# Gate and up weights fetched piece by piece in the last mixer slot, block 1's token rows fetched with block 0's, and block 0's first slice placed behind the last scores

## The reference

```python
xn = layernorm(x)
q, k, v = silu(xn @ Wq.T), silu(xn @ Wk.T), silu(xn @ Wv.T)
f = log_sigmoid(xn @ Wf.T) / 8;  s = 1 - exp(f)
# pass 1: S = S * exp(f) + k s^T;  ok = q S;  qv = softmax(ok)
# pass 2: S = S * exp(f) + s v^T;  ov = qv S
o = silu(ov);  rms = o * rsqrt(mean(o * o) + 1e-5)
attn = (rms * g_w) @ Wo.T
# feed-forward: act_quant to 8 bits by the row's largest value, weight_quant to {-1, 0, 1} / scale
gate = silu(bitlinear(xn, w_gate));  up = bitlinear(xn, w_up)
ffn = bitlinear(gate * up, w_down)
out = x + attn + ffn
```

## Time and profile before

| | |
|---|---|
| median of 3 runs | 1513.44 us (1511.06 to 1515.44) |
| the profiled execution | 1519.48 us |
| its span on the slowest core (core 7) | 1517.9 us; the other cores 1485.6 to 1512.5 us |
| PE busy / weight loads / DVE / ACT / POOL | 89% / 46% / 57% / 43% / 13% |
| 16 DMA engines, the two larger queues | 48.2% (SP's) and 5.9% (POOL's) of the span |
| slot 14 on core 7 | 793.7 to 827.8 us |
| transition on core 7 | 827.8 to about 892.4 us, where `down(0)` begins |
| feed-forward blocks behind it | 892.4 to 1517.9 us |

### The profile page before, as it was taken

How to read it: one execution, slowest core, us unless ns; L and a number is a source line. 1 busy time by engine, 2 the same in 40 slices (tenths; PEclk the granted TensorE clock), 3 DMA queues, 4 the chain that set the end, 5 groups by cost and what they waited for, 6 DMA issues and landing times.

```text
span 1517.9 us, 24194 instructions; the slowest of 8 cores (1485.6 to 1517.9 us)
## 1 busy us (share of the span) xinstructions
PE 1358.4 (89%) x7996; PEld 701.5 (46%) x7996; DVE 867.5 (57%) x1475; ACT 651.4 (43%) x1082; POOL 195.8 (13%) x225
## 2 busy tenths in 40 slices
PE   2666899878889988888898899999999999999999
PEld 1223344345556555555555344444444444444444
DVE  2455556338776667777777355554455445555543
ACT  1555322457788887877775211111111111111120
POOL 1000000011221111211212011111111011001110
PEclk9899999989999999999999999999999999999999
DMA  9898999716676766676752932323322233332322
GB/s 152 203 213 183 226 251 277 209 33 192 196 225 231 200 177 198 193 215 204 230 175 71 352 97 57 77 63 77 76 56 64 70 77 77 77 72 61 77 49 56
DMA packets 193690, 219.69 MB, mean 145 GB/s; under 512 B 125856, under 2 KB 146336, under 8 KB 192416
## 3 DMA queue, kind: packets, MB, share of 16 engines
q1 hardware_dynamic: 187664, 197.18, 48.2%
q0 software_dynamic: 5904, 20.97, 5.9%
HBM read 167.78 MB, written 29.36 MB: 130 GB/s over the span
## 4 chain that ended last, share of the span: by engine, by line
PE 64%; DMA 13%; DVE 8%; ACT 7%; issue 6%; SPq 2%; POOL 1%; DVEq 0%; ACTq 0%; POOLq 0%
PE ps L265 62%; DMA stg<-wgT 4%; DMA stg<-wuT 3%; DMA xin<-xp 2%; DMA wf<-wfT 2%; ACT b_ok L282 1%; SPq L310 1%; PE ps L270 1%; DVE STf L299 1%; ACT stg L282 1%; DVE part L418 1%; DMA xin<-xr 1%; DVE b_ok L285 1%; DVE stB L461 1%; ACT b_wo L282 1%
## 5 line engine op out<-in xcount | busy, mean ns | idle before, releaser
L265 PE MATMUL ps<-wgu,xnTb 128*128 128x512 fp8e4 x2048 | 447.3, 380 | 6.8 <-DVE gu L285 6.8
L265 PEld LDWEIGHTS ps<-wgu,xnTb 128*128 128x128 bf16 x2048 | 200.4, 98 | 248.8 <-issue 9.2
L282 ACT ACTIVATE sg<-ps,ccol 128x512 f32<-128x512 f32 x128 | 86.0, 684 | 424.1 <-PE ps L265 423.0
L265 PE MATMUL ps<-wd,qT 128*128 128x512 fp8e4 x960 | 209.6, 379 | 0.0
L285 DVE TENSOR_TENSOR gu<-ps,sg 128x512 f32<-128x512 f32 x128 | 88.3, 690 | 187.9 <-PE ps L265 178.7
L265 PEld LDWEIGHTS ps<-wd,qT 128*128 128x128 bf16 x960 | 94.0, 98 | 113.2
L282 ACT ACTIVATE stg<-stg,wsc 128x1024 f32<-128x1024 f32 x96 | 109.7, 1145 | 38.8 <-DMA stg<-wuT 17.3
L461 DVE TENSOR_SCALAR stB<-stg 128x1024 fp8e4<-128x1024 f32 x96 | 69.1, 719 | 67.7 <-ACT stg L282 59.1
L418 DVE TENSOR_REDUCE part<-stg 128x1 f32<-128x1024 f32 x64 | 77.5, 1218 | 48.6 <-DMA stg<-wgT 28.4
L265 PE MATMUL ps<-wf,xnTa 128*128 128x512 bf16 x256 | 65.4, 415 | 39.4 <-DMA wf<-wfT 27.4
L303 POOL CAST b_s<-STf 128x512 bf16<-128x512 f32 x64 | 45.7, 716 | 421.7 <-DVE STf L299 419.8
(11 more groups left out here) (139 smaller groups left out, 1933.8 us busy)
## 6 DMA issues: line engine op xcount, KB each, us to landing
stg<-wgT SPq DMA_DIRECT2D x64, 512.0 KB, 6.8
stg<-wuT SPq DMA_DIRECT2D x64, 512.0 KB, 6.2
stg<-wdT SPq DMA_DIRECT2D x64, 512.0 KB, 5.1
xin<-xr SPq DMA_DIRECT2D x32, 512.0 KB, 4.6
xin<-xp SPq DMA_DIRECT2D x16, 512.0 KB, 5.8
gu_s<-stB SPq DMA_DIRECT2D x64, 128.0 KB, 5.7
at_s<-b_wo SPq DMA_DIRECT2D x32, 256.0 KB, 2.2
wgu<-gu_s POOLq DMA_DIRECT2D x8, 1024.0 KB, 17.4
```

Source lines behind the costliest of these rows:

```text
L265: return pe(lambda e: e.matmul(out=out, lhsT=lhsT, rhs=rhs, start=start, stop=stop, skip_group_check=True), *toks, mark=mark)
L282: return sc(lambda e: e.activation(out=out, in_=in_, func=func, **kw), *toks)
```

## The change

Four edits, all around slot 14 and the transition:

1. `wv` and `wq` change places in memory, so that the four weights lie in the order in which slot 14 last reads them: `wf`, `wk`, `wq`, `wv`.
2. The eight loads of `wgu` are issued in four pairs in slot 14, each behind the last reader of the weight that lies there: slices 0 and 1 after `F_(15, 1)`, 2 and 3 after `K_(15, 1)`, 4 and 5 after `Q_(15, 1)`, 6 and 7 after `V_(15, 1)`. `F_`, `K_` and `Q_` record their last matmul as `wdone` for this.
3. `load_x(1)` moves from the transition to slot 14, right behind `load_x(0)`.
4. `gu_pe(0, 0)` moves from behind `Wo_pe(14, 1)` to directly behind `AT_(15)`.

`prep_x(1)`, which reads the rows that `load_x(1)` fetches, stays where it was.

```diff
--- before.py
+++ after.py
@@ -188,8 +188,8 @@
 
         wf = at("wf", 8192, BF16, W0)
         wk = at("wk", 8192, BF16, W0 + 16384)
-        wv = at("wv", 8192, BF16, W0 + 32768)
-        wq = at("wq", 8192, BF16, W0 + 49152)
+        wq = at("wq", 8192, BF16, W0 + 32768)
+        wv = at("wv", 8192, BF16, W0 + 49152)
         wgu = at("wgu", 65536, FP8, W0)
         wo = at("wo", 8192, BF16, WO0)
 
@@ -742,7 +742,7 @@
         def F_(c, h):
             d = B[c]
             bk = RP.take()
-            p = proj(c, bk, wf, wf_t, h)
+            d["wdone"] = p = proj(c, bk, wf, wf_t, h)
             u = U.get(("e", h))
             t = act(b_e[h], bk.ap, AF.Exp, p, u, A2_done, scale=-1.0)
             bk.put(t)
@@ -813,6 +813,7 @@
                            wq[:, kc * 1024 + col:kc * 1024 + col + 128],
                            xT[:, kc * 128:(kc + 1) * 128], kc == 0, kc == 7,
                            X[("o", c)]["xnT"], wq_t, bk.freed, mark=(kc == 7 and j == 3))
+            d["wdone"] = p
             t = act(b_QT[:, hsl(h)], bk.ap, AF.Silu, p, U.get(("QT", h)))
             bk.put(t)
             d["Q%d" % h] = t
@@ -820,7 +821,7 @@
         def K_(c, h):
             d = B[c]
             bk = RP.take()
-            p = proj(c, bk, wk, wk_t, h)
+            d["wdone"] = p = proj(c, bk, wk, wk_t, h)
             t = act(heads(b_KV[:, h * 1024:(h + 1) * 1024], 2, 0), v3(bk.ap, 2), AF.Silu, p,
                     U.get(("U", h)))
             bk.put(t)
@@ -1083,6 +1084,13 @@
         V = {}
         wl_t = []
         wd_t = []
+
+        def load_gu(g, tok):
+
+            for sl in (2 * g, 2 * g + 1):
+                wl_t.append(dma("wl%d" % sl, gp, wgu[:, sl * 8192:(sl + 1) * 8192],
+                                d_gu[:, sl * 8192:(sl + 1) * 8192], tok,
+                                store_t[0], store_t[1]))
 
         def load_x(b):
             s = b % 2
@@ -1234,6 +1242,8 @@
             up(c, 0)
             ok_ex(c, 1)
             F_(f, 1)
+            if s == NO - 2:
+                load_gu(0, B[f]["wdone"])
             qt_dv(c, 0)
             if w is not None:
                 Wo_pe(w, 0)
@@ -1273,6 +1283,7 @@
             if s == NO - 2:
                 bg_end = [stg_tok, stB_tok]
                 load_x(0)
+                load_x(1)
                 prep_x(0)
             K_(f, 0)
             bg_a()
@@ -1287,6 +1298,8 @@
             s2_cast(2)
             s2_cast(3)
             K_(f, 1)
+            if s == NO - 2:
+                load_gu(1, B[f]["wdone"])
             bg_a()
             bg_b()
             Q_(f, 0)
@@ -1295,6 +1308,8 @@
             bg_b()
             s1_tr(1, RC)
             Q_(f, 1)
+            if s == NO - 2:
+                load_gu(2, B[f]["wdone"])
             bg_a()
             bg_b()
             KT_(f, 1)
@@ -1302,6 +1317,8 @@
             bg_a()
             bg_b()
             V_(f, 1)
+            if s == NO - 2:
+                load_gu(3, B[f]["proj"])
             bg_a()
             bg_b()
 
@@ -1309,11 +1326,8 @@
         c = NO - 1
         w = c - 1
         upd_end = [("pe", pe.n), ("dv", dv.n), ("sc", sc.n), ("gp", gp.n)]
-        for sl in range(8):
-            wl_t.append(dma("wl%d" % sl, gp, wgu[:, sl * 8192:(sl + 1) * 8192],
-                            d_gu[:, sl * 8192:(sl + 1) * 8192], B[c]["proj"],
-                            store_t[0], store_t[1]))
         AT_(c)
+        gu_pe(0, 0)
         gram(w)
         ok_pe(c, 0)
         ok_dv(c, 0)
@@ -1328,7 +1342,6 @@
         Wo_el(w, 1)
         qt_dv(c, 1)
         wd_t.append(dma("wd", gp, wd, d_wd, store_t[2], B[c]["qt1"], upd_end))
-        gu_pe(0, 0)
         qT_(c, 0)
         BT_(c, 0)
         qT_(c, 1)
@@ -1337,7 +1350,6 @@
         ov_pe(c, 0)
         BT_(c, 1)
         ov_el(c, 0)
-        load_x(1)
         prep_x(1)
         gu_pe(0, 2)
         gu_el(0, 1)
```

## The result

The changed kernel takes 1507.58 us (median of 6 runs) against 1515.88 us before (6 runs), at a ratio of 0.9934 with an interval of 0.9914 to 0.9955, which is 10 us of 1515.88. Measured again beside the last experiments, it is 0.9946 (0.9925 to 0.9967), 8 us. 1505.6 us had been forecast, in a range of 1502.5 to 1510.5.

What follows compares the result with a forecast made beforehand. PE, busy 621.8 of 625.5 us from down(0) on, was taken to bound the kernel, so down(0)'s start sets its end. 6.48 + 1.64 - 0.3 = 7.8 us off the median 1513.4 gave 1505.6 us, range 1502.5 to 1510.5.

Steps and rivals of the forecast that it cites:

- The stall of slice 3: Before slice 3's up half, PE's idle 6.85 us shrinks to 1.19 us; gain 6.48 us, with slice 0's 0.66 us in it.
- The clock: Slice 3's up half, eight matmuls, runs at full clock after the shorter stall: 1.64 us more, bounds 0 to 1.64.
- Rival B: At slice 3 the clock stays low and some wait stays: gain 6.2 or 4.5 us, 1508 us; chance 0.17.
- Slice 0 ahead of `gram`: Its sixteen matmuls, moved ahead of gram and pass 1, cover the wait for mask b_at: 0.66 us gained.
- All of this costs nothing: Slices and wd, fetched from slot 14 on, land before PE wants them and delay nothing on POOL: 0 us.
- the slip of 0.3 us: Block 0's rows in slot 14 land 0.3 us late, which DVE's queue hands on to PE.
- almost done: The first pair, 2.1 MB in 6.1 us from 799.7, has nearly landed when block 0's rows are issued.
- a bound of 2.1 us: With turns by packet, block 0's rows take at most about twice 3.5 us in slot 14 and slip 2.1 us.
- rival C: No change: block 0's rows in slot 14 land 9.4 us late instead; 1514.7 us, chance 0.15.
- The reason given for the late rows: Block 1's rows took 14.28 us because their load shares the DMA engines with 12 MB of wgu and wd.
- even shares: Queues taking equal turns by packet; doubted because block 1's rows were a tenth of what moved in 14.28 us.
- D: Slower: slice 0, heading PE's queue, waits for block 0's transpose, 1 us per us beyond 828.25; 1518 us, chance 0.05.

Runs made afterwards that it cites:

- e1_rows_early: The kernel before with only load_x(1) moved, directly behind load_x(0) in slot 14; ratio 0.9975 to before.
- e4_slice0_back: The changed kernel with gu_pe(0, 0) put back behind Wo_pe(14, 1); 1511.88 us in one run.
- the six kernels: Those that fetch the first pair of slices early and leave prep_x(0) in its place; slot 14 takes 35.68 us on their mean.
- e6_pair0_later: The changed kernel with the first pair of slices issued together with the second, behind K_(15, 1); 1505.58 us in one run.
- e2_weights_early: The changed kernel with load_x(1) back in the transition and gu_pe(0, 0) back behind Wo_pe(14, 1); ratio 1.0034 to before.
- e8_wd_pieces: e2_weights_early with wd fetched as 8 loads with rows of 4 KB instead of one with rows of 32 KB; 1513.24 us in one run.
- e9_preps_later: The changed kernel with prep_x(0) moved to ahead of Q_(15, 0) and prep_x(1) to behind gu_el(0, 1); ratio 0.9988 to before.
- e10_slices_behind_transpose: e9_preps_later with slices 2 to 7 also waiting for block 0's transpose to land; ratio 0.9887 to before, 1498.20 us.

## Why the prediction was right, and where it was not

**The stall of slice 3: right.** On core 7, on which the sum was made, the transition went from 64.65 to 56.44 us, 8.2 us; 6.48 + 1.64 = 8.12 had been summed. The up half was due at 843.12 + 1.73 = 844.85 and began at 845.95, so 1.10 us stayed, where 1.19 had been worked out. `e1_rows_early` shows that the early rows alone remove the stall.

**The clock: right.** 0.94 us of idle time left eight matmuls at 1.89 us and the window at 1.00. Other runs show that it was not a near thing: 1.94 us cost nothing either, while 2.73 us cost most of the price (3.02 us), 4.42 us nearly all of it (3.38 us) and 14.14 us no more (3.27 us). Rival B did not come about.

**Slice 0 ahead of `gram`: right**, 0.66 us, shown by `e4_slice0_back`.

**"All of this costs nothing", and the slip of 0.3 us: the mechanism was right, the term of the sum was too small.** On five cores `prep_x(0)` started later than its queue let it, which the prediction had named as a sign of being wrong. Block 0's rows were late by 0.72 us on the mean (0 to 1.59; up to 2.62 on one core of the repetition), and slot 14 grew by 0.65 us, by 0.9 on the mean of the six kernels. The first pair of slices did it, shown by `e6_pair0_later`; it was not "almost done" as 6.1 us of bytes had it. The two loads took a median of 7.9 us from their issue, and the issue itself came about 0.8 us behind the last matmul of `F_(15, 1)`. The prediction had worked out a bound of 2.1 us from turns by packet and set it aside; the largest slip in the change's own profile was 1.59 us. With means over all cores the sum is 7.48 - 0.65 = 6.8 us, on the last core of before 8.2 less its slip. (In rival C a load of 8 us comes 3.1 us late, not 3.3.)

**The reason given for the late rows was wrong in kind.** The prediction laid it on 12 MB in flight, and held against even shares that the rows were a tenth of what was moved. The shares are even, but by packets: 132 to 162 while the bytes stood 7 to 1 (`e2_weights_early`), 197 to 197 in the kernel before, and the same bytes in shorter rows let the load through in about half the time (`e8_wd_pieces`). The rows were a tenth of what was moved because the stores ahead of them in SP's queue were another tenth, and the neighbour's packets were longer. The Trainium skill's rule on Arbitration ("DMA: Bandwidth & Descriptors") says just this, that a DMA engine goes round its queues packet by packet, and these runs agree with it. That the forecast stood all the same is in part luck: nothing in the reason given said what the rows would meet in slot 14, and they met only the tail of the first pair, with rows of 8 KB. It follows from turns by packet that the early weights don't relieve the rows' load: without `load_x(1)` beside them they make it worse, by 5 us.

**What the early weights do give** had not been seen. From `e1_rows_early` to `e4_slice0_back`, which differ in them alone, the transition goes from 58.93 to 57.10 us. They clear the way for the transpose of block 1, which no longer waits behind them (4.2 to 5.6 us in flight over the cores instead of 18.9 to 23.4). But they also bring the 0.9 us of slot 14 with them, so that half of these 1.8 us is left. With slice 0 the way is 63.92, 58.93, 57.10, 56.44 us: 5.0 for the rows, 1.8 for the weights, 0.7 for slice 0. This order is the one in which each pays; alone, the second and third cost 6.7 and 17.9 us.

**Rivals C and D** named real mechanisms. C's (block 0's rows pay instead) is there at 0.7 us instead of 9.4. D's price was not paid, because the second pair is issued behind block 0's transpose, as was argued; `e9_preps_later` takes that away and loses 16.6 us in the transition.

**What stays open.** The profiled spans differ by 13.2 us: 8.2 in the transition, less 0.4 in slot 14, and 5.4 because slot 14 began at 788.24 us on core 6 and at 793.69 on core 7 before. No instruction before slot 14 moved, and the same start varies from run to run of other kernels (794.07 on the last core of `e1_rows_early`, 788.45 on that of `e2_weights_early`).

The ratio's 10 us in the first comparison, and 8 in the repetition, are more than the stretches give. The spans of all cores, recorded for every run of the repetition, explain a part. The mean over the eight cores fell from 1503.0 us (11 runs) to 1496.8 (5 runs), 6.2 us, where the stretches of its profile give 7.48 - 0.96 = 6.5. The slowest core fell from 1514.2 to 1506.6, 7.6 us. So the average core gains what the stretches say, and the slowest a little more, for the cores lie closer together with the change. With `e10_slices_behind_transpose` it is the same: 15.2 us for the mean, 17.0 for the slowest, 14.3 by the stretches. In `e9_preps_later` the stretches are 2.4 us longer than before and the mean of the cores 0.9 us, while the slowest core is 2.4 us shorter. Whether the first comparison's 10 us holds more than this and spread was not settled.

## What to carry to other kernels

A small transfer beside a large one is not slowed by the bytes in flight but by its own number of packets, with those ahead of it in its own queue, times the length of the other queue's packets. So ask, for every small load and every transpose, which long-rowed load is in flight beside it and which stores stand ahead of it; issue the small one first, and let the large one wait for it where both can't be moved. And price a part of a change together with the others: here the three parts were worth 5.0, 1.8 (0.9 with what it cost in slot 14) and 0.7 us in one order, while two of them alone made the kernel slower (slice 0 in a single run).

## What the runs showed of the hardware that had not been expected

- A 128x1024 bf16 transpose took 3.1 us when no other queue was busy, 5.0 beside the tail of `wd`, 18.3 beside loads with rows of 8 KB, and 23.4 behind the 12 MB of weights. Its packets are about 250 bytes.
- A load of 512 KB took 3.5 us alone, and 18.9 to 21.6 behind two stores and beside 4 MB with rows of 32 KB, landing with it. In one stretch of 5 us the two queues moved 197 packets each.
- Waits for transfers were what made the cores differ in the transition: 61.56 to 65.75 us before, 56.43 to 56.44 with the change. In slot 14 of the kernel before neither PE nor DVE waits for a transfer, and still it is 34.11 to 35.24 us. The waits there are nearly alike, but `Q_(15, 1)` behind them took 3.10 us on core 7 and 3.62 on core 3, both above the full clock's 1.95. With the waits gone (`e9_preps_later`, `e10_slices_behind_transpose`) slot 14 is 28.18 us on all eight.
- PE's stalls of 0.93 to 1.94 us cost no clock on any core, those of 2.73 us and more cost 0.95 to 1.68 us in the eight matmuls behind them.
